# A decoder layer's prologue: constant rows of the score operands written in place, bias rows loaded to fewer partitions, and a new order of steps

## The reference, cut to what matters

```python
x = x + attn(layernorm(x))               # 16 heads of 8, causal softmax, layernorm * gamma + beta, @ Wo.T
x = x + xattn(ctx, ctx, layernorm(x))    # one head of 128, 64 context rows, biases bv, bq, bo
x = x + ffn(layernorm(x))                # 8 experts, 128 -> 512 -> 128, relu, biases b1, b2
# gates of ffn: entmax (alpha 1.5) over the 8 logits of a token; out = sum over experts of y * gate
```

## Time and profile before

| what | us |
|---|---|
| median of 3 runs | 665.8 (664.77 to 667.24) |
| the profiled execution | 664.33 |
| its span in the trace | 662.6 |
| TensorE busy | 618.6 (93%) |
| VectorE busy | 464.3 (70%) |
| ScalarE busy | 408.0 (62%) |
| GpSimd busy | 363.9 (55%) |
| mean granted TensorE clock | 0.991 |

### The profile page before, as it was taken

One profiled execution on the slowest core, in us unless ns is written; L12 is line 12 of the kernel. 1 busy time (PEld: TensorE's weight loads), 2 busy tenths in 40 slices (PEclk: granted clock), 3 DMA queues, 4 the chain that ended last, 5 costly groups with the idle time before them and its releaser, 6 DMA issues.

```text
span 662.6 us, 15729 instructions
## 1 busy us (share of the span) xinstructions
PE 618.6 (93%) x5263; PEld 459.8 (69%) x5263; DVE 464.3 (70%) x996; ACT 408.0 (62%) x780; POOL 363.9 (55%) x599
## 2 busy tenths in 40 slices
PE   5488879999999999999999999999999999998997
PEld 3355557777677767777678767777677767776775
DVE  4495984679747986689747986599557984656544
ACT  4239476755777566755766557755776567665543
POOL 8625565445663737444763746544753756464363
PEclk9889999999999999999999999999999999999999
DMA  6705100530027000630036000720045000700230
GB/s 187 230 17 169 45 4 18 127 117 4 19 45 208 10 8 14 151 107 2 18 67 191 0 20 0 162 95 2 18 98 159 2 2 6 159 2 1 55 88 16
DMA packets 39195, 43.76 MB, mean 66 GB/s; under 512 B 2922, under 2 KB 23670, under 8 KB 39158
## 3 DMA queue, kind: packets, MB, share of 16 engines
q1 hardware_dynamic: 39158, 43.28, 24.5%
HBM read 10.04 MB, written 2.10 MB: 18 GB/s over the span
## 4 chain that ended last, share of the span: by engine, by line
PE 77%; DVE 8%; ACT 6%; POOL 3%; issue 2%; DMA 2%; SPq 2%; ACTq 0%; DVEq 0%; POOLq 0%
PE h_ps L1038 10%; PE y_ps L1038 9%; PE h_ps L1040 8%; PE h_ps L1039 8%; PE y_ps L1040 8%; PE y_ps L1039 8%; DVE negmax L1657 5%; PE sbuf_m L1149 5%; PE sbuf_s L1132 3%; PE sbuf_s L1104 2%; ACT prob L1462 2%; PE sbuf_s L1149 2%; PE sbuf_s L1053 1%; PE sbuf_s L1066 1%; PE sbuf_m L1038 1%
## 5 line engine op out<-in xcount | busy, mean ns | idle before, releaser
L1773 DVE SCALAR_TENSOR_TENSOR h_lo<-h_ps,h_hi 128x512 fp32r<-128x512 f32 x256 | 172.2, 682 | 120.3 <-ACT h_hi L1481 119.4
L1481 ACT ACTIVATE h_hi<-h_ps 128x512 fp32r<-128x512 f32 x256 | 152.1, 601 | 129.7 <-PE h_ps L1040 127.7
L1038 PE MATMUL h_ps<-fT_lo,w_hi 128*128 128x512 f32 x256 | 111.6, 436 | 4.1 <-DVE fT_lo L1626 2.7
L902 POOL TENSOR_SCALAR_AFFINE_SELECT prob<-prob 128x512 f32<-128x512 f32 x128 | 79.8, 642 | 60.7 <-ACT prob L1462 57.2
L1462 ACT ACTIVATE prob<-sbuf_s 128x768 f32<-128x768 f32 x124 | 95.2, 813 | 25.7 <-PE sbuf_s L1132 25.7
L1038 PE MATMUL y_ps<-h_lo,w_hi 128*128 128x512 f32 x255 | 106.9, 419 | 1.5 <-ACT y_sb L1490 1.5
L1657 DVE TENSOR_REDUCE negmax<-sbuf_s 128x4 f32<-128x1024 f32 (+1 forms) x91 | 106.9, 1212 | 0.1
L1039 PE MATMUL h_ps<-fT_hi,w_lo 128*128 128x512 f32 x256 | 101.2, 395 | 0.0
L1040 PE MATMUL h_ps<-fT_hi,w_hi 128*128 128x512 f32 x256 | 101.1, 395 | 0.0
L1040 PE MATMUL y_ps<-h_hi,w_hi 128*128 128x512 f32 x255 | 100.8, 395 | 0.0
L1039 PE MATMUL y_ps<-h_hi,w_lo 128*128 128x512 f32 x255 | 100.7, 395 | 0.0
(11 more groups left out here) (449 smaller groups left out, 1046.2 us busy)
## 6 DMA issues: line engine op xcount, KB each, us to landing
gate_b<-gT SPq DMA_DIRECT2D x64, 256.0 KB, 4.9
stacks<-qk SPq DMA_DIRECT2D x42, 256.0 KB, 2.5
gate_b<-in_L_ffn_W_dram SPq DMA_DIRECT2D x8, 512.0 KB, 6.1
...
```

Of the source, the lines that this page charges most:

```text
L902: pool.affine_select(out=v, in_=v, compare_op=ALU.is_ge, fill=0.0, base=0, pattern=[[0, 2], [0, 2], [1, P]], channel_multiplier=-1).then_i ...
L1038: pe.matmul(out_ap, w_hi, m_lo, start=start, stop=False)
L1481: act.activation(h_hi[:, c % HB, :], h_ps[:, c % 2, :], ACT.Relu).then_inc(hhi_made, 1)
L1773: dve.scalar_tensor_tensor(out=h_lo[:, c % HB, :], in0=h_ps[:, c % 2, :], scalar=0.0, in1=h_hi[:, c % HB, :], op0=ALU.max, op1=ALU.subtrac ...
```

## The change

What it does:

- **Stacks.** The four memsets, the table in `acc` and its sixteen DMAs are gone. VectorE makes in `acc` ten small memsets (a column of cell numbers over 256 tokens), GpSimd keeps the part below the diagonal (one `affine_select` of 128x128), VectorE sums the rows and makes two small factors, and four `tensor_scalar` operations of 128x2048 write the constants of all rows into the stacks in place, two for pair 0 (one before and one behind `setup`) and two for pair 1 (step stacks 1). The DMAs of Q's and K's words wait for these (`stacks_made`).
- **Bias rows.** `b1` goes with two DMAs of 16 KB to 2 partitions of each 32. GpSimd clears the whole area first (128x1024), and step bL waits for that on SP. Pairs takes four two-tensor operations instead of two fused ones.
- **Vectors.** The four rows are issued by ScalarE's queue at its start.
- **Levelling.** The two `tensor_scalar` of 128x128 become `tensor_tensor` with a broadcast column; step xwq moves behind most of pair 0's attention on VectorE.
- **Steps anew.** All lists get other numbers. In the prologue all four w1 loads are issued ahead of the stacks' words, the split of the third w1 part, the tables kp, vp, cT 1, T1 of pair 1 and a w1 table come ahead of MAX 0, MAX 12 to 15 come ahead of PV 2, and w2 3 comes earlier on GpSimd. In the rounds TH 0 moves behind the masks of SC 4 and 5, TH 2 behind the mask of SC 8, and GV from slot 7 to slot 6 of VectorE.

```diff
-            for n, v in enumerate([gamma, beta, xbv, xbq]):
-                sp.dma_start(vec_rows[n:n + 1, :], row(v)).then_inc(wq_loaded, 16)
...
                 if ph.first:
-                    sp.wait_ge(const_made if n else const0_made, 5 if n else 2)
+                    sp.wait_ge(stacks_made[n], 2)
...
-                for j in range(NJ):
-                    r = slice(ROWS * j + 11, ROWS * (j + 1), 4)
-                    for a, dst in enumerate(stacks_of(pair)):
-                        sp.dma_start(words(dst[r, :, :]).rearrange("p g (b s) -> p (g b) s", s=S),
-                                     cell_rows[11:ROWS:4, a, :].unsqueeze(1).to_broadcast([6, 2 * NG, S]))\
-                          .then_inc(cells_loaded[pair], 16)
...
-                    sp.dma_start(whole[:, 0:2 * F], b1.rearrange("(a n) f -> a (n f)", n=2).unsqueeze(1)
-                                 .to_broadcast([NE // 2, 32, 2 * F])).then_inc(b_loaded, 16)
+                    sp.wait_ge(whole_cleared, 1)
+                    for r in range(2):
+                        sp.dma_start(whole[r:P:32, 0:2 * F], b1.rearrange("(a n) f -> a (n f)", n=2)).then_inc(b_loaded, 16)
...
+            pool.wait_ge(cells_base, 10)
+            pool.affine_select(out=row_sums, in_=row_sums, compare_op=ALU.is_ge, fill=0.0, base=0,
+                               pattern=[[-1, P]], channel_multiplier=1).then_inc(rows_kept, 1)
...
+            pool.memset(whole[:, 0:2 * F], 0.0).then_inc(whole_cleared, 1)
...
-            def first_stacks():
-                pool.memset(words(qs0), 0.0).then_inc(const0_made, 1)
-                pool.memset(words(ks0), 1.0).then_inc(const0_made, 1)
-
             def masks():
-                pool.memset(words(qs[:, :, :]), 0.0).then_inc(const_made, 1)
-                pool.memset(words(ks[:, :, :]), 1.0).then_inc(const_made, 1)
...
+            for n, v in enumerate([gamma, beta, xbv, xbq]):
+                act.dma_start(vec_rows[n:n + 1, :], v.rearrange("(a e) -> a e", a=1)).then_inc(wq_loaded, 16)
...
+            def stack_constants(n, which=(0, 1)):
+
+                q_rows, k_rows = stacks_of(n)
+                cells = cell_of.unsqueeze(1).to_broadcast([P, 2 * NG, S])
+                if n == 0 and 0 in which:
+                    dve.wait_ge(rows_kept, 1)
+                    dve.tensor_reduce(row_at, row_sums, AX.X, ALU.add).then_inc(cells_made, 1)
+                    dve.wait_ge(cells_made, 1)
+                    dve.tensor_scalar(above, row_at, 0.0, MASKED, ALU.is_ge, ALU.mult).then_inc(cells_made, 1)
+                    dve.tensor_scalar(below_11, row_at, 0.0, None, ALU.is_lt).then_inc(cells_made, 1)
+                    dve.wait_ge(cells_made, 3)
+                    dve.tensor_tensor(behind, above, below_11, ALU.add).then_inc(cells_made, 1)
+                dve.wait_ge(cells_made, 4)
+                for k in which:
+                    dst, op, by = ((q_rows, ALU.is_equal, 1.0), (k_rows, ALU.is_gt, behind))[k]
+                    dve.tensor_scalar(dst[:, :, :].rearrange("p g (b s) -> p (g b) s", s=S), cells, row_at, by, op, ALU.mult)\
+                       .then_inc(stacks_made[n], 1)
...
-                mark(dve.tensor_scalar(xwq_hi[:, :], w_in[:, 7, :], tilt[:, 1:2], None, ALU.add))
-                mark(dve.tensor_scalar(w_in[:, 7, :], w_in[:, 7, :], tilt[:, 1:2], None, ALU.add))
+                level = tilt[:, 1:2].to_broadcast([P, E])
+                mark(dve.tensor_tensor(xwq_hi[:, :], w_in[:, 7, :], level, ALU.add))
+                mark(dve.tensor_tensor(w_in[:, 7, :], w_in[:, 7, :], level, ALU.add))
...
-                    for v, w in ((b1_pairs, whole[:, 0:2 * F]), (xbo_pair, whole[:, 2 * F:2 * F + E])):
-                        ins = dve.scalar_tensor_tensor(out=v, in0=v, scalar=odd[:, 0:1], in1=w, op0=ALU.mult, op1=ALU.add)
+                    pairs = (b1_pairs, whole[:, 0:2 * F]), (xbo_pair, whole[:, 2 * F:2 * F + E])
+                    for v, w in pairs:
+                        mark(dve.tensor_tensor(v, v, odd[:, 0:1].to_broadcast(list(v.shape)), ALU.mult))
+                    settle()
+                    for v, w in pairs:
+                        ins = dve.tensor_tensor(v, v, w, ALU.add)
...
-    Step("TH", 0, "-", pool=0),
+    Step("TH", 0, "-", pool=0.5),
...
-    Step("GV", 0, "-", dve=7.01),
+    Step("GV", 0, "-", dve=6.02),
```

More of the change, by code:

```diff
@@ L78 @@
 Z_STEPS = [
[L79 to L86, removed]
+    Step("SZ", 0, "-", dve=8.5162, pool=2.75),
+    Step("NZ", 0, "-", act=12.5242),
+    Step("T1", 0, "t", pe=14.0063, act=14.0174, dve=14.0075),
@@ L91 @@
[L91 to L100, removed]
@@ L106 @@
 A_STEPS = [
[L107 to L116, removed]
@@ L166 @@
     Step("SZ", 0, "-", dve=0, pool=0),
-    Step("stacks", 0, "-", pool=0.25),
+    Step("masks", 0, "-", pool=0.25),
     Step("w1L", 0, "-", sp=0),
+    Step("NZ", 0, "-", act=0),
     Step("w1L", 1, "-", sp=0.25),
-    Step("NZ", 0, "-", act=0),
     Step("XL", 1, "-", sp=0.5),
-    Step("bL", 0, "-", sp=0.75),
-    Step("xwq", 0, "-", dve=0.25),
-    Step("RL", 0, "-", sp=1),
-    Step("T1", 0, "u", pe=0, act=0.25, dve=0.5),
-    Step("cells", 0, "-", pool=0.5, sp=1.25),
-    Step("Q", 0, "y", pe=0.25, act=0.75, dve=0.75),
@@ L300 @@
-    Step("SC", 18, "h", pe=24, act=18.5, pool=9),
-    Step("XO", 1, "y", pe=24.5, dve=20.25),
-    Step("SC", 19, "t", pe=24.25, act=18.75, pool=9.25),
-    Step("w2", 3, "-", act=19, pool=9.75),
-    Step("V", 1, "v", pe=24.75, dve=20.75),
-    Step("SA", 5, "-", dve=20.5, pool=9.5),
-    Step("NA", 2, "-", act=19.25),
+    Step("w1L", 2, "-", sp=0.75),
+    Step("xwv", 0, "m", pe=0, act=0.25, dve=0.5),
+    Step("constants", 0, "-", pool=0.5),
+    Step("xwo", 0, "u", pe=0.25, act=0.75, dve=0.75),
@@ new lines @@
+    Step("MT", 2, "v", pe=17.75, dve=14.25, sp=3.75),
+    Step("TA", 0, "y", pe=18, act=14, dve=14.5),
+    Step("MAX", 23, "s", pe=17.25, dve=13.75),
+    Step("BT", 2, "t", pe=18.25, dve=14),
+    Step("BT", 3, "m", pe=18.5, dve=14.75),
+    Step("MAX", 20, "s", pe=18.75, dve=15.25),
+    Step("w1", 0, "u", pe=19.25, act=14.75, dve=18.25),
+    Step("SA", 3, "-", dve=15, pool=6.75),
+    Step("bias", 0, "m", pe=19.5, act=14.5),
+    Step("WO", 0, "v", pe=19.75, dve=15.75),
+    Step("NA", 3, "-", act=14.25),
@@ L509, in bass_decoder_layer @@
         acc = sb("acc", [P, TOK])
-        cell_rows = acc[0:ROWS, :].rearrange("p (a s) -> p a s", a=2)
+        cell_of = acc[:, 0:S]
+        row_sums = acc[:, S:S + P]
+        row_at, behind, above, below_11 = (acc[:, S + P + k:S + P + k + 1] for k in range(4))
         gate_b = sb("gate_b", [P, NE, TOK])
@@ L565, in bass_decoder_layer @@
         const_made = sem("const_made")
-        const0_made = sem("const0_made")
+        stacks_made = [sem(f"stacks_made_{k}") for k in range(2)]
+        whole_cleared = sem("whole_cleared")
         filler_made = sem("filler_made")
@@ L589, in bass_decoder_layer @@
         nm_cleared = sem("nm_cleared")
+        cells_base = sem("cells_base")
+        rows_kept = sem("rows_kept")
         cells_made = sem("cells_made")
-        cells_loaded = [sem(f"cells_loaded_{k}") for k in range(2)]
         pool_turn = sem("pool_turn")
```

370 lines of the change are left out of this document (189 added, 181 removed).

## The result

The changed kernel takes 676.4 us (median, 675.0 to 679.4) against 665.8: slower, ratio 1.0164, 95% interval 1.0120 to 1.0207. The forecast was 660.4, faster. The interval leaves open whether the loss is over 2%. The profiled execution took 679.4 us, at a mean granted clock of 0.978, and is the slowest of the four runs; the two quickest, 675.0, had 0.988 and 0.989.

The account below looks back on a forecast made before the run. TensorE was taken to bound the rounds, waits the prologue. Prologue -8.1, rounds +2.1, phase 4 +0.5, phase 3 +0.1 gave -5.4 against 664.33: 658.9; the median, 1.5 above, 660.4 us, range 652 to 667.

Parts of the forecast that it names:

- The bias rows: Prologue: ScalarE's 4.71 us wait for b1 had slack, so the smaller load might change nothing in the sum.
- The words' issue: Prologue: Q's and K's words, held by SyncE alone, issued from about 16.4 instead of 20.42, 4 us sooner.
- The first maximum: Prologue: first maximum near 26.9 against 33.39, taken as -6.5 us, between -4.5 and -8.
- The lock-out: Prologue rival: VectorE and GpSimd block each other, some 3 us on Q's low word; 663.4 us, chance 0.14.
- To the end of the prologue: Behind the first maximum: four maxima moved ahead -1.1, earlier w2 split -0.5; prologue in all -8.1.
- The rounds: GV ahead of h_lo(7) delays TensorE 0 to 0.5 us; 0.3 taken in each of seven phases, +2.1.
- mass at 335.3: Rounds, gates: masks off the chain behind TH 0 (-1.2), SC 8's mask ahead of TH 2 (+0.6); mass was at 335.89.
- The end of the round: T2 and T3 of phase 3 shift by at most 0.7 us each with opposite signs: +0.1.
- GV stalls every round: Rounds rival: if mass comes after 336, h_lo(7) waits for all of GV, some 10 us; 668 to 675, chance 0.10.

Follow-up runs that it names:

- e3: The kernel before with only the four steady-state lists (A, X, Z, G) of the changed kernel: 678.2 us, ratio 1.0155.
- e2: The changed kernel with the four steady-state lists (A, X, Z, G) of before; new code and prologue order stay: 666.4 us, ratio 1.0000.
- e16: The kernel before with the bias rows alone changed (two transfers of 16 KB, area cleared by GpSimd first): 660.2 us, ratio 0.9890.
- e13: e4 with the bias rows loaded as before, by one transfer of 512 KB, without GpSimd's clearing: 665.9 us, ratio 0.9995.
- e4: The changed kernel's code with all the lists of before, prologue included: 660.3 us, ratio 0.9904 against the kernel before.
- e15: e2 with pair 1's stack constants moved behind MT 1 on VectorE and the pairs operations fused: 665.1 us, ratio 0.9969.
- e5: e2 with more matmuls without use in the prologue, eight instead of one ahead of WO 0 and five ahead of T3 0: 662.3 us, ratio 0.9946.
- e1: The changed kernel with GV put back in slot 7 of VectorE instead of 6: 673.5 us, ratio 1.0074.
- e8: The changed kernel with list X (LG, TH, GV, GT, YM) of before: 670.5 us, ratio 1.0034.
- e12: e8 with NA 2 on ScalarE and T3 on all engines back behind MT 1 at the round's end: 669.7 us, ratio 1.0041.

## Why the prediction was wrong

The forecast was -5.4 us; +10.6 were measured. The new lists of the rounds cost 10 us (e3) where the forecast had 2.7 for rounds and phases 3 and 4; the prologue with the new code gains nothing at the median (e2) where it had -8.1. Both parts failed, in these steps:

- **The bias rows** were costed at nothing ("the bias rows may not have delayed anything: ScalarE's 4.71 us had slack, and it would change nothing in the sum"). That step failed: they are the whole gain of the code, 6 to 7 us (e16), and they are what shortened the landing of K's words from a median of 5.4 us (8.0 the last) to 2.6.
- **The words' issue** was costed as the gain ("the issue is held by SyncE alone"). The words did go out at 15.75 (forecast 16.4) and were there at 22 (25 to 27). But an earlier issue alone gains nothing while the bias load is there (e13). With the old order the new code does gain 6 us (e4), near the -6.5; that is luck, since the gain comes of the bias rows.
- **The first maximum**: forecast 26.9, measured 31.01. The chain through the w1 splits and NZ 1 was named; its duration was summed from undisturbed rows. The lock-out had been put as a rival on VectorE, with Q's low word as the victim; it fell on GpSimd (e15: 3.25 us at NZ 1; with the clock, 4.8 at the first maximum). Q's low word lost hardly anything (14.96 against 14.50). The four constants took 1.29, 2.21 and 2 x 1.27: the 1.36 taken was right, and the second of the four, 2.21, ran beside GpSimd's memset of 7.17 to 8.98.
- **To the end of the prologue**: forecast -1.6 more, measured a loss of the 2.4 us won, and 1.15 on top. The clock's falls at 80 to 90 and 100 to 110 were no term of the sum at all, though the earlier trace rows show one (0.77 from 20 to 32) in the kernel before; with fillers against them e2 gains 4 us (e5).
- **The rounds**: +0.3 a phase forecast, 1.3 measured. The step that failed is "mass at 335.3": the masks did move into GpSimd's idle time, and took their 1.2 us off the chain behind TH 0 as forecast, but TH 0 started 0.43 us later into the round than before, and SC 8's mask with the waits around it cost 0.8 instead of 0.6. So `mass` came 15.85 us into the round, as before, and `h_lo(7)` behind the whole of GV. Of the 0.43, 0.31 lie in one operation of VectorE ahead of TH 0 (L1724), which takes 0.74 beside the two masks where before it took 0.43 without them. GV's slot costs 0.65 to 0.7 (e1), the rest of list X some 0.2 (e8). The end of the round, costed at +0.1 in phase 3 only, costs 0.15 to 0.35 in every round (e12), and 0.4 more lie in list Z or A and were no term of the sum.
- **The rival that came true** is "GV stalls every round", at the place named (VectorE's slot, TensorE waiting for `h_lo(7)`), with half of its price, beside other causes of the loss that weren't on the list. The condition that it set, `mass` after 336, was not met (335.90 on that scale): GV's length was enough. Its chance of 0.10 and the range's upper end of 667 were too low: a rival with eight phases behind it needed more weight than a prologue that is passed once.
